# Storing the results of a graph attention layer in halves of an image instead of quarters

## The reference

```python
alpha = _bn_relu(jnp.einsum('bchw,oc->bohw', x, wa), ga, ba, ma, va)
sigma = _bn_relu(jnp.einsum('bchw,oc->bohw', x, ws), gs, bs, ms, vs)
att = jnp.einsum('bkn,bkm->bnm', af, sf)
att = jax.nn.softmax(jnp.where(adj, att, NEG), axis=2)
h_s = jnp.einsum('bnm,bcm->bcn', att, xf).reshape(b, c, h, w)
Gc = jnp.einsum('bcn,bdn->bcd', xf, xf)
catt = jax.nn.softmax(jnp.where(cadj, Gc, NEG), axis=2)
h_p = jnp.einsum('bcd,bdn->bcn', catt, xf).reshape(b, c, h, w)
h_prime = jax.nn.elu(h_s + h_p)
return (1.0 - gama) * x + gama * h_prime
```

## Time and profile before

| | |
|---|---|
| Median of three runs | 413.83 us |
| The three runs | 413.4, 413.83, 425.62 us |
| The profiled execution, time on the device | 416.75 us |
| Its span in the profile | 415.0 us |
| Mean granted PE clock, share of full | 0.964 |
| Bytes moved | 137.74 MB, of them read 103.26, written 33.55 |
| Busy: PE, DVE, ACT, POOL | 364.1, 315.5, 305.8, 291.6 us |

### The profile page before, as it was taken

The page is one execution under the profiler, slowest core; times in us unless marked ns, Lnnn a source line. Parts: engine busy times, 40 slices in busy tenths (PEclk is TensorE's granted clock), DMA queues, the critical chain, the costliest instruction groups (busy, mean ns, idle before and its releaser), DMA issues.

```text
span 415.0 us, 14346 instructions
## 1 busy us (share of the span) xinstructions
PE 364.1 (88%) x5487; PEld 277.5 (67%) x5488; DVE 315.5 (76%) x1072; ACT 305.8 (74%) x900; POOL 291.6 (70%) x198
## 2 busy tenths in 40 slices
PE   5977998989998999999899999999989898999783
PEld 1546767666766867676686767677676667767662
DVE  1166978778787688879768887978788697888775
ACT  2178686868878497887849788787869678686761
POOL 2007686787868588787858878788868858787861
PEclk9889999999999899999989999999999899999778
DMA  8999999999999899999999999999999999985213
GB/s 274 414 368 404 315 344 357 366 359 347 364 346 385 292 358 366 388 364 351 356 317 337 382 385 360 363 378 383 342 367 358 365 307 367 341 297 202 103 53 152
DMA packets 40613, 137.74 MB, mean 332 GB/s; under 512 B 3296, under 2 KB 3552, under 8 KB 36448
## 3 DMA queue, kind: packets, MB, share of 16 engines
q1 hardware_dynamic: 40256, 136.76, 91.4%
q10 hardware_dynamic: 288, 0.07, 0.1%
HBM read 103.26 MB, written 33.55 MB: 330 GB/s over the span
## 4 chain that ended last, share of the span: by engine, by line
PE 32%; DMA 30%; DVE 20%; ACT 9%; issue 7%; SPq 0%; DVEq 0%; ACTq 0%
DMA upper<-x_t_dram 28%; PE gb L468 17%; PE z L468 11%; ACT score L281 6%; DVE probs L374 5%; DVE elu L389 5%; PE tr L543 3%; DVE z L383 3%; ACT z L301 3%; DMA x<-x_dram 2%; DVE gb L404 1%; DVE band L400 1%; DVE row_inv L370 1%; DVE pair_inv L420 1%; DVE catt L421 1%
## 5 line engine op out<-in xcount | busy, mean ns | idle before, releaser
L468 PEld LDWEIGHTS z<-probs_t,upper 64*128 64x128 f32 x2304 | 155.6, 191 | 44.6 <-issue 28.8
L468 PE MATMUL z<-probs_t,upper 64*128 64x128 f32 (+1 forms) x2304 | 173.5, 284 | 5.1 <-ACT probs_t L292 2.4
L247 POOL TENSOR_TENSOR blend<-elu,blend 128x1024 f32<-128x1024 f32 x62 | 146.2, 2358 | 9.5 <-POOL elu L243 0.4
L243 POOL TENSOR_SCALAR elu<-elu,vec,mix 128x1024 f32<-128x1024 f32 x62 | 74.0, 1193 | 98.5 <-DVE elu L389 98.5
L308 ACT ACTIVATE elu<-z 128x512 f32<-128x512 f32 x128 | 69.6, 597 | 60.6 <-PE z L468 60.6
L389 DVE SCALAR_TENSOR_TENSOR elu<-elu,z 128x512 f32<-128x512 f32 x124 | 79.5, 683 | 28.7 <-ACT elu L308 28.3
L301 ACT ACTIVATE z<-x,catt 128x512 f32<-128x512 f32 x128 | 83.6, 693 | 14.2 <-DVE catt L421 14.1
L281 ACT ACTIVATE score<-score,neg_max 128x128 f32<-128x128 f32 x256 | 86.2, 337 | 7.4 <-DVE neg_max L365 7.3
L383 DVE SCALAR_TENSOR_TENSOR z<-near,catt,z 128x512 f32<-128x512 f32 x128 | 90.3, 751 | 1.5 <-ACT z L301 1.5
L237 POOL TENSOR_SCALAR blend<-x,mix 128x1024 f32<-128x1024 f32 x64 | 72.0, 1126 | 6.5 <-DMA x<-x_dram 6.5
L468 PE MATMUL gb<-x,wt 128*32 128x256 f32 (+2 forms) x720 | 65.1, 480 | 2.5 <-DMA x<-x_dram 2.5
(11 more groups left out here) (49 smaller groups left out, 145.0 us busy)
## 6 DMA issues: line engine op xcount, KB each, us to landing
x<-x_dram SPq DMA_DIRECT2D x32, 1024.0 KB, 9.1
near<-x_near_dram SPq DMA_DIRECT2D x64, 512.0 KB, 7.8
out_dram<-blend SPq DMA_DIRECT2D x62, 512.0 KB, 8.0
upper<-x_t_dram SPq DMA_DIRECT2D x16, 1152.0 KB, 8.4
upper<-x_t_dram SPq DMA_DIRECT2D x16, 1024.0 KB, 7.9
out_dram<-blend SPq DMA_DIRECT2D x4, 256.0 KB, 2.1
const<-constants_dram SPq DMA_DIRECT2D x1, 291.5 KB, 12.0
const<-constants_dram SPq DMA_DIRECT2D x1, 128.0 KB, 2.2
```

The source lines that it names most:

```text
L243: nc.gpsimd.tensor_scalar(elu[s % 2][:, :, :], elu[s % 2][:, :, :], vec[:, V_GAMA:V_GAMA + 1], mix[:, 1:2], ALU.mult, ALU.add).then_inc(ga ...
L247: nc.gpsimd.tensor_tensor(blend[s % BLENDS][:, :, :], elu[s % 2][:, :, :], blend[s % BLENDS][:, :, :], ALU.add).then_inc(blend_done, 1)
L468: return nc.tensor.matmul(o, l, r, start=start, stop=stop, skip_group_check=True, **kw)
```

## The change

Two quarters share a buffer. There are three buffers of half an image (128 x 2 x 1,024 elements, `PAIRBUFS`) in place of four of a quarter, so 24 KB per partition in place of 16 KB. `blend(s)` is the quarter's part of a buffer, and POOL and DVE write into it as before. SP stores at odd t only, for both quarters of step t - 2 and the one before it: 256 rows of 4 KB, 1,024 KB in one transfer. `keep_x(s)` waits for the store of the pair that had the same buffer. The last two steps are stored as before, in four small transfers.

```diff
-BLENDS = 4
+PAIRBUFS = 3
...
-        blend = [sb(f"blend{i}", [P, HALF, QN]) for i in range(BLENDS)]
+        halves = [sb(f"blend{i}", [P, HALF, HALVES]) for i in range(PAIRBUFS)]
+
+        def blend(s):
+            return halves[s // 2 % PAIRBUFS][:, :, s % 2 * QN:(s % 2 + 1) * QN]
...
                 if s < TAIL:
                     sp.wait_ge(blend_done, s + 1)
-                    sp.dma_start(out_img[b, :, :, q * QN:(q + 1) * QN], blend[s % BLENDS][:, :, :])\
-                        .then_inc(stored[s % BLENDS], 16)
+                    sp.dma_start(out_img[b, :, :, (q - 1) * QN:(q + 1) * QN], halves[s // 2 % PAIRBUFS][:, :, :])\
+                        .then_inc(signal, 16)
...
-                if real(t - 2):
+                if real(t - 2) and (t % 2 == 1 or t - 2 >= TAIL):
                     store(t - 2)
...
-                if s >= BLENDS:
-                    pool.wait_ge(stored[s % BLENDS], 16 * (s // BLENDS))
-                nc.gpsimd.tensor_scalar(blend[s % BLENDS][:, :, :], xs[b % XBUFS][:, :, cols(q)], mix[:, 0:1],
+                if s >= 2 * PAIRBUFS:
+                    pool.wait_ge(stored[s // 2 % PAIRBUFS], 16 * (s // 2 // PAIRBUFS))
+                nc.gpsimd.tensor_scalar(blend(s), xs[b % XBUFS][:, :, cols(q)], mix[:, 0:1],
```

More of the change, by code:

```diff
@@ L110, in graph_attention @@
         upper_in = [[sem(f"upper_in{j}{i}") for i in range(2)] for j in range(2)]
-        stored = [sem(f"stored{i}") for i in range(BLENDS)]
+        stored = [sem(f"stored{i}") for i in range(PAIRBUFS)]
         pads_done = sem("pads_done")
@@ L182, in store @@
                 b, q = s // QUARTERS, s % QUARTERS
+                signal = stored[s // 2 % PAIRBUFS]
                 if s < TAIL:
                     sp.wait_ge(blend_done, s + 1)
-                    sp.dma_start(out_img[b, :, :, q * QN:(q + 1) * QN], blend[s % BLENDS][:, :, :])\
-                        .then_inc(stored[s % BLENDS], 16)
+                    sp.dma_start(out_img[b, :, :, (q - 1) * QN:(q + 1) * QN], halves[s // 2 % PAIRBUFS][:, :, :])\
+                        .then_inc(signal, 16)
                 else:
@@ L189, in store @@
                         sp.wait_ge(tail_done, 2 * (s - TAIL) + h + 1)
-                        sp.dma_start(out_img[b, :, h, q * QN:(q + 1) * QN], blend[s % BLENDS][:, h, :])\
-                            .then_inc(stored[s % BLENDS], 16)
+                        sp.dma_start(out_img[b, :, h, q * QN:(q + 1) * QN], blend(s)[:, h, :])\
+                            .then_inc(signal, 16)
             sp.dma_start(const[:, 0:C_BAND], constants[:, 0:C_BAND]).then_inc(ident_in, 16)
@@ L222, in _ @@
                     load_by_key(b + 2, 0)
-                if real(t - 2):
+                if real(t - 2) and (t % 2 == 1 or t - 2 >= TAIL):
                     store(t - 2)
-            for i in range(BLENDS):
-                sp.wait_ge(stored[i], 16 * (STEPS // BLENDS + (i >= TAIL % BLENDS)))
+            for i in range(PAIRBUFS):
+                whole = len(range(i, TAIL // 2, PAIRBUFS))
+                sp.wait_ge(stored[i], 16 * (whole + (4 if i == TAIL // 2 % PAIRBUFS else 0)))
         @block.gpsimd
@@ L246, in add_elu @@
                 pool.wait_ge(gama_done, s + 1)
-                nc.gpsimd.tensor_tensor(blend[s % BLENDS][:, :, :], elu[s % 2][:, :, :], blend[s % BLENDS][:, :, :],
+                nc.gpsimd.tensor_tensor(blend(s), elu[s % 2][:, :, :], blend(s),
                                         ALU.add).then_inc(blend_done, 1)
@@ L394, in add_tail @@
                 dve.wait_ge(keep_done, s + 1)
-                nc.vector.scalar_tensor_tensor(blend[s % BLENDS][:, h, :], z[s % 2][h][:, :], vec[:, V_GAMA:V_GAMA + 1],
-                                               blend[s % BLENDS][:, h, :], ALU.mult, ALU.add).then_inc(tail_done, 1)
+                nc.vector.scalar_tensor_tensor(blend(s)[:, h, :], z[s % 2][h][:, :], vec[:, V_GAMA:V_GAMA + 1],
+                                               blend(s)[:, h, :], ALU.mult, ALU.add).then_inc(tail_done, 1)
             def gram_pick(b):
```

## The result

The changed kernel is slower: 423.81 us (median of four runs, 420.12 to 426.02) against 414.82 us (413.40 to 425.62), a ratio of 1.0216 with a 95% interval of 1.0154 to 1.0279. The loss is real; its size is 1.3 or 2.2%, some 5 or 9 us, and whether it is above 2% stays open. A ratio compares the quicker runs of both kernels, those within 1.5% of the fastest of each, so it can differ a little from the ratio of the medians. I had forecast 412 us and a range of 404 to 420.

What follows compares the result with a forecast made beforehand. The prediction took the DMA engines, full at 354 GB/s, as the bound. Its terms, -3 (packets) -1.3 (once) -1 (waits) +3.3 (loads without a store) = -2.0, put the 413.83 us median at 411.8, rounded 412 us; range 404 to 420.

Steps and rivals of the forecast that it cites:

- The DMA engines set the pace: Outside the clock's dips, full engines at 354 GB/s bound each image, with PE about 1 us per image behind.
- Part 1: Stores with 4 KB rows in place of 2 KB: 7,936 packets for 15,872, 3 us gained, bounds 0 and 4.0.
- Part 2: Two stores move behind an `upper`: lighter queue in front gains 1.3 us once, plus 1 us of PE's waits.
- Part 3: Loads of x and `near` lose the stores beside them and run slower: 3.3 us lost, between 0 and 8.8.
- Rival 3: Each image's loads meet a store only twice and slow down: up to 431 us; sign under 345 GB/s; chance 0.13.
- Rival 1: Packets are free because the memory's bytes set the DMA rate: 412.5 to 414 us; chance 0.20.
- Rival 2: Lighter queue lands each `upper` 1.3 us earlier, so the kernel falls into PE's pace: 399 us; chance 0.17.
- Rival 4: A transfer waits for a buffer; needs a landing of 18 us where 10 are expected; chance nearly nothing.
- slower by over 2%: Whole kernel above 422.1 us, most of the rival with slower loads; chance 0.10.
- the fall of the share: Sign of being wrong: DMA share in 50 to 370 us well below 98%, so the engines weren't the bound.
- the landings and PE's wait: Signs for the moved stores: `upper` landing shorter than 7.9 to 8.4 us, PE's wait for it below 12.0 us.

Runs made afterwards that it cites:

- single move: Pair buffers, rows of 2 KB; against the kernel before, only the store of t = 0 mod 4 goes one step later, behind the `upper` of q = 1: 0.9702.
- pairs_behind_x: The changed kernel's stores, each issued one step later, behind x and before the next `near` and `upper`, with four pair buffers: 1.0417 against the kernel before.
- after: The changed kernel in its first series, against the kernel before: median 423.81 us, ratio 1.0216; its packet times come from one profiled execution.

## Why the prediction was wrong, point by point

**"The DMA engines set the pace."** This is the step that failed, and the others hang on it. I had read the digit 9 and a share of 98.4% as saturation. A packet of 8 KB that takes 481 ns counts as busy just like one of 309, so the share can't tell a full pipe from a slow one. The chain of waits said what was true: one image is the landing of `upper`, some 8 us, plus 15.4 us. I had its 24.03 us and wrote that it said "the same from the other side", when it was a bound of its own. An early issue of that one load, which changes no byte, took 2 to 4% off the time of the kernel before (0.9783 and 0.9632 there, 0.9671 and 0.9598 with the pair stores), and moved 367 GB/s at a share of 96.0% where I had taken 354 for the limit. Without half of the stores the kernel took 0.976 and not the 0.89 to 0.93 of a kernel bound by bytes.

**Part 1, the packets: -3 us.** Direction and size aren't refuted, but nothing of it was seen: 0.9983 with 4 KB rows and a store in every step, 1.0199 against 1.0216 and 1.0131 in the new one. Engine time that nobody waits for is worth nothing, and in a sum for a chain through a landing the -3 had no place.

**Part 2, the stores behind `upper`: -1.3 -1 us.** The sign was wrong. The place of the stores is what made the kernel slower: 1.0199 with the old rows in the new places, 0.9968 with every store in its old place. "Between two `upper` transfers the queue holds the same bytes as before" is right, but they are now issued in the first 8 to 9 us of each stretch, and the packets of both loads got slower, from 432 and 464 ns to 481 and 499. PE's wait for `upper` grew by 4.7 us in one trace of the changed kernel and by 1.7 in the other, where I had put a gain. That the slow packets carry the whole loss, and why the load of q = 1 is slower with the same gap in front of it, is not shown; the cause stays open there. What I did see rightly is that a lighter queue in front of the load of q = 1 is a gain: 0.976 without the stores of the even steps, 0.970 with the single move.

**Part 3, the loads without a store beside them: +3.3 us.** The term with the right sign, for a wrong reason. The slow stretches of the earlier trace rows followed the issues of `upper` at 186.75 and 198.35; I noticed that ("after the `upper` of 186.75") and looked for the missing store. Without any store the packets of the two loads are still slow, 384 and 432 ns. And the loads that lost their neighbour, x and `near`, became quicker, 165 ns for a packet of 4 KB in place of 174.

**The rivals.** Rival 3 (slower) had the sign, but its mechanism, a lower rate of all loads, did not happen: x and `near` became quicker, and the rate of 350 stayed above the 345 that I had named as its sign. Rival 1 held in its first half as far as one could see: no gain of the packets showed. Rival 2, the fall into PE's pace, did not happen in the changed kernel, only where `upper` of q = 1 was issued early: 401 us, near the 399 that I had worked out for it. Rival 4 stayed out: POOL waited for no store.

**The numbers.** 423.81 is 2.9% above my 412 and above the 420 of the range; 1.0131 times the 413.83 of before would be 419.3, just inside. I had given 0.10 to slower by over 2%, and a loss by the place of the stores was not among the rivals. Of the signs that I had named for being wrong, the fall of the share was weak (96.8% in one trace, 98.2% in the other); the landings and PE's wait were the better ones.

## What to carry to other kernels

A high busy share of the DMA engines is not a bound by itself: ask for the landing of the transfer that the chain of waits goes through, and try on paper what happens if it is issued earlier. When transfers are merged or moved, look at when they go out and not only at how many bytes lie in between: here the place alone cost 1 to 2% with the same bytes, the same rows and the same buffers. Compare more than one trace before a small difference is put down to what a trace shows: in two of these the end of the kernel differed by 5 us, with PE's clock at 0.77 and 0.98 there. The first edit to try here was neither larger stores nor fewer packets but two lines that issue the critical load before an unrelated wait.

## What the runs showed of the hardware

- A load of `upper` that started 1.0 to 1.3 us after its issue took 367 to 481 ns for a packet of 8 KB and 432 to 499 for one of 9 KB; one that started 2 us or more after it took 312 to 359 and 352 to 365. In between, at 1.6 and 1.7 us, 9 KB took 436 and 469. The start alone doesn't fix the number: at about 1 us the 8 KB packets were at 367 in `pairs_behind_x` and at 481 in `after`. Why such loads are slow wasn't found out. It isn't the stores alone (384 and 432 ns without them), nor the size of their rows (463 and 491 with 2 KB).
- A store of one channel per partition (128 rows of 4 KB, 16 KB apart) took a median of 429.19 us beside 413.69 of the kernel before; one of 64 partitions with both channels (rows 8 KB apart) 418.74 beside 419.41. One of the six runs of the first was at 417.96, so what the cut costs is not settled.
- Without stores, loads alone and at the kernel's own rhythm: 272 GB/s at a share of 80.7%. With the early load: 367 GB/s at 96.0%. The kernel before: 354 GB/s at 98.4%.
- Runs of one kernel differ by up to 4.5% (410.5 to 429.7 us in 75 runs of the kernel before, on four chips), and much of it goes with PE's mean granted clock (correlation 0.81). After the last load that clock was 0.98 in one trace and 0.77 in another, and the stretch from there to the end 44 and 50 us.
